# MLP block of an adaLN layer: the last 64 values and gates share a weight tile, GpSimd adds the two channel halves ahead of the layer-norm sums, and the norm of the next chunk starts at the head of a chunk

## The reference, cut to what matters

```python
# x: (2, 2048, 256); after an adaLN attention block, a feed-forward part of two layers:
def _layer(x, wqkv, qs, ksc, wo, lg, lb, w1, b1, w2, b2):
    ...                                            # windowed attention, 8 heads, windows of 128
    x = x + o @ wo
    h = shift_token(x)                             # second half of the channels comes from token t-1
    mu = h.mean(-1, keepdims=True)
    var = h.var(-1, keepdims=True)
    h = (h - mu) / jnp.sqrt(var + 1e-05) * lg + lb
    h = h @ w1 + b1                                # 256 -> 2 * 682
    a, g = jnp.split(h, 2, axis=-1)                # 682 values, 682 gates
    h = a * jax.nn.gelu(g, approximate=False)
    x = x + h @ w2 + b2                            # 682 -> 256
    return x
```

## Time and profile before

| | |
|---|---|
| median of three runs | 4878.4 us |
| the profiled execution, its own time | 4882.99 us |
| its span, first to last instruction | 4881.1 us |
| mean granted TensorE clock | 0.971 of full speed |
| busy: TensorE, VectorE, ScalarE, GpSimd | 94%, 70%, 45%, 56% of the span |
| MLP phases, layer 0 and layer 1 | about 3796 to 4049 us and 4598 to 4850 us |

### The profile page before, as it was taken

How to read it: one execution, slowest core, us unless ns; L and a number is a source line. 1 busy time by engine, 2 the same in 40 slices (tenths; PEclk the granted TensorE clock), 3 DMA queues, 4 the chain that set the end, 5 groups by cost and what they waited for, 6 DMA issues and landing times.

```text
span 4881.1 us, 65202 instructions
## 1 busy us (share of the span) xinstructions
PE 4565.5 (94%) x21552; PEld 2792.1 (57%) x21552; DVE 3426.1 (70%) x4564; ACT 2212.1 (45%) x3535; POOL 2728.9 (56%) x1172
## 2 busy tenths in 40 slices
PE   7999999999999999999999999858999897999898
PEld 5555555555555555555555555426766675777576
DVE  7887878778788788787787787565555454666354
ACT  5444444444444444444444444325665343656442
POOL 3655656566556665675666565606666223666322
PEclk9999999999999999999999999979999998999898
DMA  2000000000000000000000000010000100000001
GB/s 65 1 5 5 2 6 1 6 6 1 6 5 2 5 1 6 6 1 6 5 2 6 5 2 2 1 56 1 1 1 1 36 1 18 1 1 1 1 0 35
DMA packets 56826, 37.55 MB, mean 8 GB/s; under 512 B 32572, under 2 KB 55056, under 8 KB 56464
## 3 DMA queue, kind: packets, MB, share of 16 engines
q1 hardware_dynamic: 56464, 33.02, 2.3%
HBM read 28.54 MB, written 4.19 MB: 7 GB/s over the span
## 4 chain that ended last, share of the span: by engine, by line
POOL 48%; issue 26%; PE 13%; DVE 7%; ACT 4%; POOLq 1%; DMA 0%; DVEq 0%; SPq 0%; ACTq 0%
POOL accp L708 36%; PE psum L1705 4%; POOL lp L730 4%; PE psum L1580 3%; POOL accp L704 3%; POOL rnorm L720 2%; POOL qk_u L725 2%; DVE ssq L1180 1%; ACT lp L894 1%; PE psum L1626 1%; ACT qk_sq L878 1%; PE psum L1718 1%; DVE qk_w L1192 1%; DVE lneg L1206 1%; PE psum L411 1%
## 5 line engine op out<-in xcount | busy, mean ns | idle before, releaser
L708 POOL TENSOR_TENSOR accp<-accp,prob 128x1024 f32<-128x1024 f32 x640 | 1618.9, 2530 | 684.3 <-ACT prob L848 651.9
L848 ACT ACTIVATE prob<-psum 128x1024 f32<-128x1024 f32 x1024 | 1042.7, 1026 | 1547.4 <-PE psum L1431 1395.8
L1076 DVE TENSOR_REDUCE mx<-psum 128x1 f32<-128x512 f32 x1984 | 1276.0, 684 | 420.3 <-PE psum L1402 354.7
L1442 PE MATMUL psum<-prob,vv 128*64 128x512 f32 x4096 | 996.0, 607 | 0.0
L1430 PE MATMUL psum<-qhh,klh 128*128 128x512 f32 x2048 | 829.4, 405 | 39.8 <-issue 20.7
L1431 PE MATMUL psum<-qlm,kh 65*128 65x512 f32 x2048 | 818.0, 399 | 0.0
L1402 PE MATMUL psum<-klh,qhh 128*128 128x512 f32 x1984 | 711.3, 419 | 14.2 <-DVE mx L1076 10.0
L1402 PEld LDWEIGHTS psum<-klh,qhh 128*128 128x128 f32 x1984 | 347.9, 190 | 413.9 <-DVE mx L1076 245.4
L1442 PEld LDWEIGHTS psum<-prob,vv 128*64 128x64 f32 x4096 | 249.5, 136 | 513.1 <-issue 370.2
L1430 PEld LDWEIGHTS psum<-qhh,klh 128*128 128x128 f32 x2048 | 392.2, 191 | 199.8 <-issue 87.2
L1431 PEld LDWEIGHTS psum<-qlm,kh 65*128 65x128 f32 x2048 | 391.7, 191 | 91.7 <-issue 7.0
(11 more groups left out here) (190 smaller groups left out, 6534.1 us busy)
## 6 DMA issues: line engine op xcount, KB each, us to landing
rot_l<-const_rot SPq DMA_DIRECT2D x2, 2048.0 KB, 8.5
out<-lpT SPq DMA_DIRECT2D x32, 128.0 KB, 1.8
wqkv_l<-L_ffn_wqkv SPq DMA_DIRECT2D x4, 768.0 KB, 9.7
w_l<-L_ffn_w SPq DMA_DIRECT2D x4, 682.0 KB
wqk<-L_attn_Wq SPq DMA_DIRECT2D x32, 64.0 KB, 2.1
wqk<-L_attn_Wk SPq DMA_DIRECT2D x32, 64.0 KB, 2.0
wv_p<-L_attn_Wv SPq DMA_DIRECT2D x16, 128.0 KB, 2.2
wo_p<-L_attn_Wo SPq DMA_DIRECT2D x16, 128.0 KB, 2.0
```

The source lines that it names most:

```text
L708: pool.tensor_tensor(acc_p[cp][:], first[:], prob[kt % PRING][:], ALU.add).then_inc(pool_sum, 1)
L848: act.activation(prob[t % PRING][:], psum[:, S_BANK + 2 * (t % 2):S_BANK + 2 * (t % 2) + 2, :].rearrange("p a b -> p (a b)"), ACT.Exp, sca ...
L1076: dve.tensor_reduce(mx4[:, j // CHUNKS, j % CHUNKS:j % CHUNKS + 1], ps, AX_X, ALU.max).then_inc(ring_free, 1)
L1442: mm = pe.matmul(psum[j * DH:(j + 1) * DH, O_BANK, :], vv[:, kt, s * DH:(s + 1) * DH], prob[t % PRING][:, j * T:(j + 1) * T], start=(kt == ...
```

## The change

The hidden units are cut anew: four tiles of 128, one of 106 and one of 64 (`TWIN`). The weights' columns are laid out so that the last 64 values and the last 64 gates stand side by side. For the sixth tile `up` makes one bank whose partitions 0 to 63 are values and 64 to 127 are gates, with 6 matmuls in place of 12; ScalarE reads the gates from partitions 64 on (`gate_row`, `gate_bank`). No padding is left, so the two clearing instructions go. The weights come in more DMAs (16 a layer in place of 11) and are split in 8 parts in place of 7.

For every chunk but the first of a layer, GpSimd adds the two halves before the sums over channels: `shifted_sum` writes `x_sum` from `xf`, `square_sum` writes over the squares. TensorE's sums then take one float32 matmul each (`sum_mean`, `sum_variance`). The mean moves ahead of `up(1)`; the variance stands behind `up(2)` and ahead of `down(0)`. ScalarE's squares move between `gl(1)` and `ug_h(1)`, and `NORM_AT` goes from 3 to 2, which moves the square root and the reciprocal to tile 2 and the gain and the splitting to tile 3. GpSimd's loop over the chunks is written out.

```diff
-HID_TILES = [(o, min(P, HID - o)) for o in range(0, HID, P)]
+TWIN = P // 2
+FULL_TILES = (HID - TWIN) // P
+HID_TILES = [(o, min(P, HID - TWIN - o)) for o in range(0, HID - TWIN, P)] + [(HID - TWIN, TWIN)]
...
-        QK_B, V_B, OL_B, NORM_AT = 4, 6, 7, 3
+        QK_B, V_B, OL_B, NORM_AT = 4, 6, 7, 2
...
+        def gate_row(t):
+            return TWIN if t == HT - 1 else 0
+        def gate_bank(t):
+            return 2 + t % 2 if t == HT - 1 else 4 + t % 2
+        def sum_mean(pe, n, done):
+            pe.wait_ge(ln_c, n + 1)
+            pe.wait_ge(x_summed, done)
+            pe.matmul(psum[:, 0, :], ones_ln[:], x_sum[:], start=True, stop=True).then_inc(ln_mu, 1)
+        def sum_variance(pe, n, par, done):
+            pe.wait_ge(sq_summed, done)
+            pe.wait_ge(ln_sd, n + 1)
+            pe.matmul(psum[:, 1, :], ones_ln[:], lns[par][:, 0, :], start=True, stop=True).then_inc(ln_var, 1)
...
-        W2_PARTS = [(0, 3, P), (3, HT - 1, P), (HT - 1, HT, HID_LAST)]
+        W2_PARTS = [(0, 2, P), (2, FULL_TILES, P)] + [(t, t + 1, HID_TILES[t][1]) for t in range(FULL_TILES, HT)]
...
-                with pool.Fori(0, ALL_CHUNKS) as c:
+                def shifted_sum(c):
+                    pool.wait_ge(ln_mu, MLP_N[l] + c)
+                    lo, hi = (xf[:, h, columns(c // CHUNKS, c % CHUNKS * T, T, shifted=h)] for h in range(HALVES))
+                    pool.tensor_tensor(x_sum[:], lo, hi, ALU.add).then_inc(x_summed, 1)
+                def square_sum(c):
+                    pool.wait_ge(ln_sq, MLP_N[l] + c + 1)
+                    sq = lns[c % 2]
+                    pool.tensor_tensor(sq[:, 0, :], sq[:, 0, :], sq[:, 1, :], ALU.add).then_inc(sq_summed, 1)
+                shifted_sum(1)
+                for c in range(ALL_CHUNKS):
                     for t, (o, size) in enumerate(HID_TILES):
+                        if t == 1 and c + 1 < ALL_CHUNKS:
+                            square_sum(c + 1)
                         gated_low((l * ALL_CHUNKS + c) * HT + t, t, size)
+                        if t == 3 and c + 2 < ALL_CHUNKS:
+                            shifted_sum(c + 2)
...
-                        act.activation(gl[t % 2][0:size, :], psum[0:size, 4 + t % 2, :], ACT.Gelu, bias=vec_b1[0:size, 1, t:t + 1]).then_inc(gelu_done, 1)
+                        rows = slice(gate_row(t), gate_row(t) + size)
+                        act.activation(gl[t % 2][0:size, :], psum[rows, gate_bank(t), :], ACT.Gelu, bias=vec_b1[rows, 1, t:t + 1]).then_inc(gelu_done, 1)
+                        if has_next and t == 1:
+                            ln_square(act, q0 + c + 1, 1 - par)
                         if has_next and t == NORM_AT:
                             ln_deviation(act, q0 + c + 1, 1 - par)
...
                         act.activation(ug_h[t % 3][0:size, :], uf[t % 2][0:size, :], ACT.Copy).then_inc(ug_hi, 1)
-                        if has_next and t == 1:
-                            ln_square(act, q0 + c + 1, 1 - par)
...
-                    for j, bank in ((0, 2 + t % 2), (1, 4 + t % 2)):
+                    for j in range(2 if gate_row(t) == 0 else 1):
                         for h in range(HALVES):
...
                     for t in range(1, HT):
+                        if has_next and t == 1:
+                            sum_mean(pe, q0 + c + 1, l * (ALL_CHUNKS - 1) + c + 1)
                         up(m, q0 + c, par, t)
+                        if has_next and t == NORM_AT:
+                            sum_variance(pe, q0 + c + 1, 1 - par, l * (ALL_CHUNKS - 1) + c + 1)
                         if t >= 2:
                             down(m, t - 2)
-                        if has_next and t == 1:
-                            ln_mean(pe, q0 + c + 1, shifted_src(c + 1))
-                        if has_next and t == NORM_AT - 1:
-                            ln_variance(pe, q0 + c + 1, 1 - par)
```

More of the change, by code:

```diff
@@ L202, in adaln_block @@
         raw = ExitStack()
-        w1_l = sb("w1_l", [P, HALVES, HID_COLS], at=raw)
+        w1_l = sb("w1_l", [P, HALVES, 2 * HID], at=raw)
         w2_l = sb("w2_l", [P, HT, D], at=raw)
         raw.close()
-        w1_low = sb("w1_low", [P, HALVES, HID_COLS], F32R, at=ffn)
+        w1_low = sb("w1_low", [P, HALVES, 2 * HID], F32R, at=ffn)
         w2_low = sb("w2_low", [P, HT, D], F32R, at=ffn)
-        w1_h = sb("w1_h", [P, HALVES, HID_COLS], F32R, at=ffn)
+        w1_h = sb("w1_h", [P, HALVES, 2 * HID], F32R, at=ffn)
         w2_h = sb("w2_h", [P, HT, D], F32R, at=ffn)
@@ L260, in adaln_block @@
         ln_r = sem("ln_r")
+        x_summed, sq_summed = sem("x_summed"), sem("sq_summed")
         w_in = [sem(f"w_in{s}") for s in range(2)]
@@ L635, in load_mlp @@
                 for h in range(HALVES):
[L636 to L639, removed]
+                    src = w1[at_l, h * P:(h + 1) * P, :].rearrange("o p (j n) -> (o p) j n", j=2)
+                    plain = HID - TWIN
+                    for lo, hi, at in ((0, plain, 0), (plain, HID, 2 * plain)):
+                        sp.dma_start(w1_l[:, h, at:at + 2 * (hi - lo)].rearrange("p (j n) -> p j n", j=2), src[:, :, lo:hi]).then_inc(l1_in, 16)
+                full = FULL_TILES * P
+                sp.dma_start(w2_l[:, 0:FULL_TILES, :], w2[at_l, 0:full, :].rearrange("o (k p) n -> p (o k) n", p=P)).then_inc(l1_in, 16)
+                for t in range(FULL_TILES, HT):
+                    o, size = HID_TILES[t]
+                    sp.dma_start(w2_l[0:size, t, :], w2[at_l, o:o + size, :].rearrange("o p n -> (o p) n")).then_inc(l1_in, 16)
                 for dst, src in ((vec_g, ln_g), (vec_b, ln_b), (vec_b2, b2)):
@@ L642, in load_mlp @@
                 for j in range(2):
-                    sp.dma_start(vec_b1[:, j, 0:HT - 1], b1[at_l, j * HID:j * HID + full].rearrange("o (k p) -> p (o k)", p=P)).then_inc(l1_in, 16)
-                    sp.dma_start(vec_b1[0:HID - full, j, HT - 1:HT], b1[at_l, j * HID + full:(j + 1) * HID].rearrange("o p -> p o")).then_inc(l1_in, 16)
+                    sp.dma_start(vec_b1[:, j, 0:FULL_TILES], b1[at_l, j * HID:j * HID + full].rearrange("o (k p) -> p (o k)", p=P)).then_inc(l1_in, 16)
+                    for t in range(FULL_TILES, HT):
+                        o, size = HID_TILES[t]
+                        lo = gate_row(t) * j
+                        sp.dma_start(vec_b1[lo:lo + size, j, t:t + 1], b1[at_l, j * HID + o:j * HID + o + size].rearrange("o p -> p o")).then_inc(l1_in, 16)
             load_attention(0)
@@ L1160, in _ @@
             dve.wait_ge(msk_ok, 1)
-            for z in (xf[:, :, 0:1], xf[:, :, N + 1:N + 2],
-                      w1_h[:, :, 2 * HID:].bitcast(F32), w1_low[:, :, 2 * HID:].bitcast(F32)):
+            for z in (xf[:, :, 0:1], xf[:, :, N + 1:N + 2]):
                 dve.memset(z, 0.0)
@@ L1266, in _ @@
                 m0, q0 = l * ALL_CHUNKS, MLP_N[l]
-                dve.wait_ge(l1_in, (l + 1) * (16 * 11))
+                dve.wait_ge(l1_in, (l + 1) * MLP_IN)
                 def gain(h):
@@ L1693, in pe_mlp_prologue, with up_tile @@
                     ln_variance(pe, q0, 0)
+                def up_tile(w, h, j, t):
+                    o = HALVES * (HID - TWIN) if gate_row(t) else j * (HID - TWIN) + t * P
+                    return w[:, h, o:o + P]
                 def up(m, n, par, t):
@@ L1699, in up @@
                     pe.wait_ge(ug_done, m * HT + t + 1)
-                    for j, bank in ((0, 2 + t % 2), (1, 4 + t % 2)):
+                    for j in range(2 if gate_row(t) == 0 else 1):
                         for h in range(HALVES):
-                            cols = slice(j * HID + t * P, j * HID + (t + 1) * P)
-                            high, low = w1_h[:, h, cols], w1_low[:, h, cols]
+                            high, low = (up_tile(w, h, j, t) for w in (w1_h, w1_low))
                             for a, (w, src) in enumerate(((high, hn_h), (low, hn_h), (high, hn_l))):
-                                mm = pe.matmul(psum[:, bank, :], w, src[par][:, h, :],
+                                mm = pe.matmul(psum[:, gate_bank(t) if j else 2 + t % 2, :], w, src[par][:, h, :],
                                                start=(h == 0 and a == 0), stop=(h == HALVES - 1 and a == 2))
```

8 lines of the change are left out of this document (4 added, 4 removed).

## The result

Four runs of the changed kernel took 4846.14 to 4851.34 us, median 4849.7; the kernel before has a median of 4882.1 over four (one more run was made beside them). The ratio is 0.9937, with a 95% interval of 0.9915 to 0.9960: 0.6% faster, or 32.4 us between the medians. The profiled execution took 4851.34 us, 31.6 less than the profiled one before.

A forecast was written before the change was run, and what follows sets the result against it. TensorE's own stream was taken to bound the MLP. Per chunk, 3.11 + 0.51 us gained less waits of 0.67 and 1.95 left 1.00; over two layers 18 us, giving 4861 us, range 4841 to 4878.

The forecast's parts named there:

- my likeliest case: Whole kernel: time within 0.5% (24 us) of the kernel before, not distinguishable from no change; chance 0.63.
- D: MLP: VectorE loses a second turn to GpSimd, `down(4)` waits 2.99 us, the change gives nothing, 4873 us; chance 0.12.
- B: MLP: both new TensorE waits stay hidden, gain 53 us, 4825 us; chance 0.06.
- A: MLP: VectorE keeps its turn through `hn_h` and `hn_l`, `shifted_sum` goes behind; gain 30 us, 4848 us; chance 0.20.
- What was removed: TensorE in the MLP: sixth tile's six matmuls, half of mean and variance, 3.11 us per chunk with a successor.
- the light wait of `down(4)`: TensorE ahead of `down(4)` in a layer's seventh chunk, without `shifted_sum`: stall 0.91 us with restart.
- The wait of the variance: TensorE ahead of the variance waits for GpSimd's `square_sum`: stall 0.58 us, about 0.67 with restart.
- The wait of `down(4)`: TensorE ahead of `down(4)` waits for `ug_l(4)`: 1.95 us with restart in six chunks a layer, 0.91 in the seventh.
- the price of a turn: GpSimd's `shifted_sum` gets in between VectorE's norm instructions, as the two engines alternate, delaying the next by 1.04 us.
- The sum: MLP chunks of both layers: gains less new waits total 18.9 us; less 1 us elsewhere, 18 us.
- the rest: Outside the main terms: DMA issues, weight splitting, written-out loop; 1 us lost over both layers, bounds -3 and +4.
- Rival C: MLP: TensorE's stalls drop the clock to half for 3.4 us, costing 1.7 us each; 4885 or 4909 us; chance 0.08.

The follow-up runs named there:

- e1: Changed kernel with GpSimd's `shifted_sum` moved from tile 3 to tile 2: periods 27.10 to 27.12 us, median 4834.3 us, ratio 0.9901 to the kernel before.
- e6: Changed kernel with `shifted_sum` done twice in a row, except for the first of a layer: periods 28.64 us, three per layer 30.2; one execution 4875.6 us.
- e9: Kernel before with only the norm's new places, halves still summed by TensorE: periods 28.81 to 28.85 us; one execution 4876.1 us.
- e4: Changed kernel with the halves added by TensorE again, no sums on GpSimd: periods 28.27 to 28.30 us; one execution 4857.4 us.
- e7: Kernel before with only the weights split in 8 parts and GpSimd's loop written out: MLP period 29.30 us; one execution 4870.3 us.
- e3: Changed kernel with the layer norm's order and sums as before, keeping the shared last tile and written-out loop: periods 29.31 to 29.33 us, ratio 0.9986.
- e2: Changed kernel with the variance's sum behind `down(0)` instead of ahead of it: periods 27.73 to 27.77 us; one execution 4839.5 us.

## Why the prediction was right, and where it was off

The measured 4849.7 us lies in the range, 11 us below my 4861. The gain was forecast at 18 us, and between the medians it is 32.4; 4.7 us of the difference belong to terms of my sum, told below; the rest lies outside the chunks. The direction holds; my likeliest case was a gain within 0.5%, and the measured one, 0.63% with an interval of 0.40 to 0.85%, lies across that bound.

**The mechanism was right.** Both new waits stand where they were put, on `square_sum` and on `ug_l(4)`; the one on `hn_l` is gone; the seventh chunk of a layer is shorter than the others; the clock is full in the MLP. D gave 29.3, B 25.7, A 27.3 in every chunk: none of them is what the profile has. Experiments e1 and e6 show that it is the turn, and not the rows of VectorE alone, that makes the ordinary chunk longer than the seventh.

**What was removed.** 3.11 us a chunk: confirmed by its parts, since e9 has the period that is left without the `hn_l` wait (28.82, forecast 28.8), and e4 (28.28) the one that follows from it with 1.39 less and the light wait of `down(4)` more.

**The wait of the variance** was put at 0.58 and is 0.47. The term that was off is the hop from ScalarE to GpSimd, 0.16 by the earlier trace rows, now 0.07 (3877.63 to 3877.70). I had the written-out loop at nothing; e7 shows 0.08 from it alone.

**The wait of `down(4)`** was put at 1.95 with the restart and is 1.51 + 0.11 = 1.62. The term that was off is the price of a turn, 1.04, measured 0.83: I gave `shifted_sum` the 1.29 us of a subtraction, and it takes 1.09 when nothing holds it (e1). It ends 0.95 us after the `hn_h` ahead of it, where I had 1.15. `square_sum`, which writes over its input, does take 1.29. Another 0.08 is the hop. With the 0.09 of the variance's hop these make 0.4 us a chunk, which is 28.32 against 27.93.

**The sum.** 23.6 us in the MLP's chunks in place of 18.9. Of the 4.7 between them 3.9 are the ten ordinary periods (10 x 0.39); the first and the seventh period and the last chunk make the rest. The remaining 8 us of the difference between the two profiled executions are not the sum's. 3.9 us lie ahead of the first `gl`, 1.9 in each layer. In layer 0 the clock was half in other places: the prologue's mean took 3.73 us before and 1.96 after, its variance 3.09 and 1.98, while `up(0)` gave 0.95 back (4.54 and 5.49 us to the first `gl`). This too comes and goes: e9, with the old prologue, has 20.0 us in layer 0 and 21.9 in layer 1. 5.5 us lie in the windowed attention, where I had put 1 us more, bounds -3 and +4. The parts alone don't give them (e7), and the changed kernel's second profile has 0.3 in their place. So "the rest" was mis-sized, in a part of the time that differs between two executions of one kernel; nothing in the prediction foresaw these 8 us, and that the whole time stayed in the range with them is partly luck. That e3 is 0.14% faster (0.04 to 0.23%) with some 3 us gained in the MLP leaves room for some microseconds outside it that I can't place.

**Rival C** had 0.08 and did not occur in the changed kernel, whose wait is 1.51 us. e2 and e6 show that it was near: with distances of 2.11 and 2.43 the clock fell once and four times a layer, and even e3, with two shorter ones, has one fall.

**The two rules.** The exclusive lock of the Trainium skill (SBUF — State Buffer, "SBUF: two separate sides") was the safer guide to A. For instructions with two SBUF inputs the trace agrees: `hn_l` was shut out while GpSimd's sum ran (1.46 us in place of 0.75, e6). `hn_h`, which has one SBUF tensor as its input, was shut out as well (1.31 in place of 0.48); the prediction had that from the earlier trace rows. The Trainium skill's "~2× slower" (GPSIMD Engine Reference, "Engine selection") would make a two-input instruction of this size 1.50 us, an estimate from the 0.75 of the earlier trace rows; the rows have 1.09 and 1.29, and these decide.

## What to carry to other kernels

A matmul taken from a TensorE-bound loop is worth its time only if the next thing it waits for is early too: six matmuls less gave 0 alone and 0.54 with the norm moved. Work that goes to GpSimd should be placed beside VectorE instructions that the trace shows undisturbed (here the reciprocal), since beside others (here `hn_h`, the gain and `hn_l`) each engine waits out the other's instruction. One SBUF input is no sign of safety: the reciprocal and `hn_h` both have one. The same sum cost 0.83 us in one place and nothing one tile earlier. Where the whole time of a program scatters by more than the step in hand, read the period of the loop in question.

## What the runs showed of the hardware

- GpSimd's float32 addition on 128x512 took 1.09 us into another tensor (`x_sum`, e1) and 1.29 written over one of its inputs (`square_sum`); the cause was not looked for.
- VectorE's reciprocal took 3.35 us both with and without a GpSimd sum beside it, and the sum its shortest time, 1.09.
- A GpSimd instruction in a hardware loop, whose waits count with the loop, started 0.16 us after ScalarE's end; written out, with waits on constants, 0.08 (e7).
- Two pipelined VectorE instructions (the second `hn_h` starts 0.08 us before the first one's end) don't keep a waiting GpSimd instruction out.
- The granted clock fell for 3.4 us inside an otherwise dense stretch of matmuls after distances of 2.11 and 2.43 us between two of them, not each time (in two of twelve and eight of twelve chunks), and never after the 1.74 of the changed kernel (24 chunks in two profiles); a fall cost 1.56 us. In e3, with no distance as long, its one fall came behind distances of 1.23 and 0.86 us, 2.1 us apart (starts of matmuls at 4713.27, 4714.50, 4715.77 and 4716.63).
